# Sorting for top-k on one core: GpSimd's share of the second payloads goes to one half in the streams, and the products behind the softmax move to GpSimd and ScalarE

## The reference

```python
y = silu(x @ sg_w) * (x @ su_w) @ sd_w              # shared perceptron
for i in range(16):
    gate_feature = x * pe[i] @ gate_w + gate_b       # 625 x 768
    gate_weight, gate_idx = top_k(gate_feature, 384)
    gate_weight = softmax(gate_weight)
    gathered = take_along_axis(x, gate_idx)
    u = gathered * gate_weight
    y = y + silu(u @ eg_w[i]) * (u @ eu_w[i]) @ ed_w[i]
```

## Time and profile before

| | |
|---|---|
| median of 3 runs | 7316.7 us (7311.38 to 7317.13) |
| profiled execution | 7314.8 us |
| its span, first to last instruction | 7313.0 us |
| granted TensorE clock, mean | 0.938 |
| busy: PE, DVE, ACT, POOL | 6048.6, 5625.4, 2711.6, 3137.3 us |

### The profile page before, as it was taken

One profiled execution on the slowest core, in us unless ns is written; L12 is line 12 of the kernel. 1 busy time (PEld: TensorE's weight loads), 2 busy tenths in 40 slices (PEclk: granted clock), 3 DMA queues, 4 the chain that ended last, 5 costly groups with the idle time before them and its releaser, 6 DMA issues. The chain is left out here.

```text
span 7313.0 us, 76698 instructions
## 1 busy us (share of the span) xinstructions
PE 6048.6 (83%) x16985; PEld 3132.3 (43%) x16985; DVE 5625.4 (77%) x6713; ACT 2711.6 (37%) x4185; POOL 3137.3 (43%) x3512
## 2 busy tenths in 40 slices
PE   7989988888787878787878787878787878788888
PEld 5545544444343434343434343434343434344454
DVE  3011012999899989898999898999999999998860
ACT  0000000444444444444444444444444444444341
POOL 2233033545454545354545454545454545454440
PEclk9989999999999989899999899999999999999999
DMA  3355364000000000000000000000000000000101
GB/s 87 115 150 147 116 141 135 20 14 14 14 14 14 14 14 14 14 14 14 14 14 14 14 14 14 14 14 14 14 14 14 14 14 14 14 14 14 59 20 47
DMA packets 118210, 262.95 MB, mean 36 GB/s; under 512 B 39164, under 2 KB 49922, under 8 KB 117682
## 3 DMA queue, kind: packets, MB, share of 16 engines
q1 hardware_dynamic: 70322, 180.18, 6.9%
q0 software_dynamic: 47360, 77.17, 4.7%
HBM read 222.43 MB, written 34.58 MB: 35 GB/s over the span
## 5 line engine op out<-in xcount | busy, mean ns | idle before, releaser
L1107 PE MATMUL mask_ps<-key,neg_ident 125*125 125x480 f32 (+7 forms) x4128 | 1929.0, 588 | 717.8 <-DVE key L1383 711.5
L1309 ACT COPY mask_ps<-key 125x960 f32<-125x960 f32 (+7 forms) x1136 | 952.5, 838 | 1762.8 <-DVE pay L1425 1383.8
L1205 POOL TENSOR_TENSOR pay<-pay_rest,pay 125x360 int32<-125x360 int32 (+11 forms) x1104 | 882.0, 799 | 1472.8 <-DVE pay L1408 1471.0
L1107 PEld LDWEIGHTS mask_ps<-key,neg_ident 125*125 125x125 f32 x4128 | 745.0, 196 | 1680.7 <-DVE key L1383 1203.4
L1408 DVE COPY_PREDICATED pay<-mask_ps,pay 125x480 f32<-125x480 int32 (+5 forms) x1104 | 1229.8, 1114 | 116.8 <-PE mask_ps L1107 80.1
L1198 POOL TENSOR_TENSOR pay_rest<-pay 125x360 int32<-125x360 int32 (+11 forms) x1104 | 878.1, 795 | 812.4 <-DVE pay L1425 512.2
L1374 DVE TENSOR_TENSOR key<-mask_ps,key 125x480 f32<-125x480 f32 (+5 forms) x1104 | 1084.4, 982 | 40.4 <-PE mask_ps L1107 35.0
L1383 DVE TENSOR_TENSOR key<-mask_ps,key 125x480 f32<-125x480 f32 (+5 forms) x1104 | 1087.7, 985 | 8.3
L1107 PE MATMUL mask_ps<-key_top,neg_ident 125*125 125x480 f32 (+3 forms) x1472 | 613.7, 543 | 317.9 <-DVE key_top L1383 303.8
L1425 DVE COPY_PREDICATED pay<-mask_ps,pay_rest 125x600 f32<-125x600 int32 (+9 forms) x1104 | 832.2, 754 | 39.7
L1323 ACT COPY pay_rest<-pay 125x600 f32<-125x600 f32 (+9 forms) x1104 | 678.6, 615 | 425.3 <-DVE pay L1425 232.6
(11 more groups left out here) (178 smaller groups left out, 5855.2 us busy)
## 6 DMA issues: line engine op xcount, KB each, us to landing
w_rel<-L_gnn_W SPq DMA_DIRECT2D x16, 2304.0 KB, 23.4
w_exp<-L_ffn_ed_w SPq DMA_DIRECT2D x16, 2304.0 KB, 8.4
messages_dram<-y_out SPq DMA_DIRECT2D x16, 1875.0 KB
w_exp<-L_ffn_eg_w SPq DMA_DIRECT2D x16, 1152.0 KB, 5.3
w_exp<-L_ffn_eu_w SPq DMA_DIRECT2D x16, 1152.0 KB, 7.8
root_w<-L_gnn_root SPq DMA_DIRECT2D x2, 2304.0 KB
w_exp<-L_ffn_sg_w SPq DMA_DIRECT2D x4, 1152.0 KB, 5.8
w_exp<-L_ffn_su_w SPq DMA_DIRECT2D x4, 1152.0 KB, 8.5
```

The lines of the kernel that those rows point to most:

```text
L1107: last = pe.matmul(mask, neg_ident[0:TP, 0:TP], operand, start=False, stop=True, skip_group_check=True)
L1205: pool.tensor_tensor(second, shares(pay_was(u))[1].bitcast(I32), first, ALU.subtract).then_inc(pays_taken, 1)
L1309: act.copy(seed_of(u), compared(u)[0]).then_inc(seeded, 1)
```

## The change

Three edits. First, `shares` learns the unit and gives GpSimd 4/8 instead of 3/8 below `APART`; above it stays 3/8. Second, the five multiplications at the turn's end leave VectorE: GpSimd multiplies exponential by payload (`weigh`) at the beginning of the next turn, ScalarE multiplies by the inverted sum (`scale`) behind the seed of unit 4, and VectorE keeps only the reciprocal (`invert`), which goes ahead of unit 2 of the next turn. Third, the work beside the units starts at unit 4 instead of unit 1 (`WEIGH` is 3), since its inputs are ready only then.

```diff
-def shares(view):
+def shares(view, u):
     dim = next(d for d in range(1, len(view.shape)) if view.shape[d] > 1)
-    cut = view.shape[dim] - max(1, view.shape[dim] * 3 // 8)
+    eighths = 4 if UNITS[u][0] < APART else 3
+    cut = view.shape[dim] - max(1, view.shape[dim] * eighths // 8)
...
+        WEIGH = 3
...
-            for u in range(1, NU - 3):
+            for u in range(WEIGH + 1, NU - 3):
...
-                    spot = 1 + next(n for n, end in enumerate(ends) if end * whole >= made * passing)
+                    spot = WEIGH + 1 + next(n for n, end in enumerate(ends) if end * whole >= made * passing)
...
+            def weigh(e):
+                pool.wait_ge(pays_done, e * NU + NU)
+                pool.wait_ge(pays_taken, e * SUMS[NU] + SUMS[NU])
+                for t in range(NT):
+                    pool.wait_ge(exp_ready, e * NT + (t + 1))
+                    pool.tensor_tensor(mlp_in[:, t, :], mlp_in[:, t, :], last_pays[:, 0:KTOP, t],
+                                       ALU.mult).then_inc(weighted, 1)
...
+            def scale(e):
+                act.wait_ge(inv_ready, e + 1)
+                for t in range(NT):
+                    act.wait_ge(weighted, e * NT + (t + 1))
+                    act.activation(mlp_in[:, t, :], mlp_in[:, t, :], ACT.Copy,
+                                   scale=exp_sum[:, t:t + 1]).then_inc(u_ready, 1)
...
+            def invert(e):
+                dve.wait_ge(exp_ready, e * NT + NT)
+                dve.reciprocal(exp_sum[:, :], exp_sum[:, :]).then_inc(inv_ready, 1)
+
             def sort(i, last_one=False):
                 for u in range(1, FIRST[APART]):
+                    if u == WEIGH - 1 and not (isinstance(i, int) and i == 0):
+                        invert(i - 1)
                     larger_keys(i, u)
...
-                dve.wait_ge(exp_ready, i * NT + NT)
-                dve.reciprocal(exp_sum[:, :], exp_sum[:, :]).then_inc(inv_ready, 1)
-                dve.wait_ge(inv_ready, i + 1)
-                dve.wait_ge(pays_done, i * NU + NU)
-                dve.wait_ge(pays_taken, i * SUMS[NU] + SUMS[NU])
-                settle(dve, sort_waits)
-                for t in range(NT):
-                    dve.scalar_tensor_tensor(mlp_in[:, t, :], mlp_in[:, t, :], exp_sum[:, t:t + 1],
-                                             last_pays[:, 0:KTOP, t], ALU.mult, ALU.mult).then_inc(u_ready, 1)
```

More of the change, by code:

```diff
@@ L1196, in add_pays @@
                     pool.wait_ge(pays_taken, i * SUMS[NU] + SUMS[NEEDS[u]])
-                first, second = [shares(side)[1].bitcast(I32) for side in payloads(u)[0:2]]
-                pool.tensor_tensor(shares(pay_was(u))[1].bitcast(I32), first, second, ALU.add).then_inc(pays_added, 1)
+                first, second = [shares(side, u)[1].bitcast(I32) for side in payloads(u)[0:2]]
+                pool.tensor_tensor(shares(pay_was(u), u)[1].bitcast(I32), first, second, ALU.add).then_inc(pays_added, 1)
             def take_pays(i, u):
-                first, second = [shares(side)[1].bitcast(I32) for side in payloads(u)[0:2]]
+                first, second = [shares(side, u)[1].bitcast(I32) for side in payloads(u)[0:2]]
                 pool.wait_ge(moved, i * MOVES[NU] + (MOVES[u] + 1))
                 pool.wait_ge(pays_added, i * SUMS[NU] + (SUMS[u] + 1))
-                pool.tensor_tensor(second, shares(pay_was(u))[1].bitcast(I32), first, ALU.subtract).then_inc(pays_taken, 1)
+                pool.tensor_tensor(second, shares(pay_was(u), u)[1].bitcast(I32), first, ALU.subtract).then_inc(pays_taken, 1)
+            def weigh(e):
[5 more added lines that the diff above has]
+                                       ALU.mult).then_inc(weighted, 1)
             def sort(i, todo):
+                if not (isinstance(i, int) and i == 0):
+                    weigh(i - 1)
                 for u in range(NU):
@@ L1213, in sort @@
                         take_pays(i, ahead)
+                    if u == WEIGH and not (isinstance(i, int) and i == 0):
+                        pool.wait_ge(weighted, i * NT)
                     if SHARED[u]:
@@ L1322, in copy_pays @@
                 else:
-                    act.copy(shares(pay_was(u))[0], shares(first)[0]).then_inc(pay_copied, 1)
+                    act.copy(shares(pay_was(u), u)[0], shares(first, u)[0]).then_inc(pay_copied, 1)
+            def scale(e):
[4 more added lines that the diff above has]
+                                   scale=exp_sum[:, t:t + 1]).then_inc(u_ready, 1)
             def sort(i, todo, last_one=False):
@@ L1327, in sort @@
                     seed(i, u + 1)
+                    if u == WEIGH and not (isinstance(i, int) and i == 0):
+                        scale(i - 1)
                     copy_pays(i, u)
@@ L1421, in second_pays @@
                     elif SHARED[u]:
-                        smaller, mask, was = [shares(side)[0] for side in (smaller, mask, was)]
+                        smaller, mask, was = [shares(side, u)[0] for side in (smaller, mask, was)]
                     dve.wait_ge(moved, i * MOVES[NU] + (MOVES[u] + 1))
@@ L1450, in sort @@
                 second_pays(i, NU - 1)
[L1451 to L1459 removed]
             larger_keys(0, 0)
             smaller_keys(0, 0)
[L1463 removed]
+            sort(0)
+            with dve.Fori(1, NEXP - 1) as i:
                 sort(i)
             sort(NEXP - 1, last_one=True)
+            invert(NEXP - 1)
 def output(nc, ffn, tiles, chunks, ident, ones, x1_dram, y_tok, m1, m1_loaded, out):
```

6 lines of the change are left out of this document (4 added, 2 removed).

## The result

The changed kernel takes 7275.8 us (median of 4 runs, 7263.2 to 7280.8), the kernel before 7316.9 in the same comparison (7311.4 to 7322.9). The ratio is 0.9935, with a 95% interval of 0.9922 to 0.9948: faster by 0.65%. The forecast was 7220 us. The time lies inside the range of 7150 to 7285 and on the foretold side, but 56 us above the number.

What follows compares the result with a forecast made beforehand. VectorE was taken to bound 15 of 16 turns, TensorE mostly the last. Terms -3.3 - 5.2 + 0.5 + 0.7 + 0.8 = -6.5 us a turn, -97 over 15, +1 in the last: 7220 us, range 7150 to 7285.

Steps and rivals of the forecast that it cites:

- the share: Second payloads in the streams (units 0 to 55): GpSimd's larger part saves VectorE 5.8 us a turn, 5.2 counted.
- the products start later: Perceptron work from unit 4: +0.5 us denser products, +0.7 low clock at the start, +0.8 GpSimd late, each turn.
- the turn's end, with what moves: Between turns: 6.27 us falls to a 2.7 us seed wait; less the reciprocal, 3.3 us saved at 15 ends.
- Turn 0: First pass of the expert loop, counted among the 15 turns that were each to lose 6.5 us.
- The last turn: Sixteenth pass, mostly TensorE's: payloads' saving -3 us, products lost to its first steps +4, together +1.
- VectorE's work: Per turn: second payloads 5.8 us less, five multiplications (4.16 us) gone, reciprocal of 0.19 us kept.
- New operations on GpSimd and ScalarE: Turn's start: five GpSimd products at 1.0 us, five ScalarE scalings at 0.474, all hidden, GpSimd even at twice the price.
- The narrow place that I named: Unit 3's payload copy, queued behind ScalarE's five scalings: just hidden; at twice the price 2 us a turn.
- GpSimd late at unit 33: GpSimd's two `xs` tiles move from unit 30 to 32, making unit 33's first payload about 0.8 us late.
- The slower rival: Low clock reaches into the products, 3.5 us lost a unit; with five units more, 7480 us; chance 0.05.
- The rival with fewer low stretches: New order fills units without a product; a third of the 167.5 us of mask waits goes: 7164; chance 0.2.
- three signs of being wrong: VectorE waiting over 1 us for GpSimd in the streams, clock near 0.5 beyond unit 8, last turn over 408 us.

Runs made afterwards that it cites:

- e1: Kernel before with only the new share of one half for GpSimd in the streams; 7210.3 us, ratio 0.9835.
- e9: Kernel before with two extra unused matmuls in each unit where TensorE has no product; 7220.6 us, ratio 0.9866.
- e8: e1 with two extra unused matmuls in each unit where TensorE has no product; 7165.8 us, ratio 0.9784.
- e5: e1 with the perceptron's work started at unit 4 in all turns but the first, old turn's end kept; 7324.7 us, ratio 1.0002.
- e15: e5 with two extra unused matmuls in each unit where TensorE has no product; 7164.7 us, ratio 0.9788.
- e4: Changed kernel with turn 0 placing its perceptron work from unit 1 again; 7258.4 us, ratio 0.9904.
- e7: e4 with two extra unused matmuls in each unit where TensorE has no product; 7120.4 us, ratio 0.9722.
- e18: Changed kernel, turn 0 still late, with two extra unused matmuls in each unit where TensorE has no product; 7132.8 us, ratio 0.9732.
- e11: e7 with ScalarE making the next turn's unit 1 seed behind the first exponential instead of the fifth; 7121.1 us, ratio 0.9729.
- e13: e11 with two turns in VectorE's loop body, so half of the jumps are gone; 7102.7 us, ratio 0.9698.
- e6: e4 with the other turns' perceptron work started at unit 3 instead of unit 4; 7213.6 us, ratio 0.9851.
- e10: e4 with two extra unused matmuls in only six of the units without a product; 7201.1 us, ratio 0.9846.

## Why the prediction fell short

The runs give each term of the sum, in us of an ordinary turn (means of turns 1 to 14), once with the clock as the kernels leave it and once held (sums from the unrounded means):

| term | forecast | measured | at a held clock |
|---|---|---|---|
| the share | -5.2 | -6.8 (before to e1) | -3.5 (e9 to e8) |
| the products start later | +0.5 + 0.7 + 0.8 | +6.6 (e1 to e5) | 0.0 (e8 to e15) |
| the turn's end, with what moves | -3.3 | -3.6 (e5 to e4) | -3.6 (e15 to e7) |
| sum | -6.5 | -3.8 (before to e4) | -7.2 (e9 to e7) |

**The products start later: this step failed.** I charged 2.0 us for it: 0.5 for denser products, 0.7 for the low clock at the start and 0.8 for GpSimd. The mask waits further on I let stand as they were. Beside the share it costs 6.6 us: with the new order other units are empty, the clock is low at other products, and masks come late behind them. Proof is the pair e1 and e5 (+6.6 us a turn) beside e8 and e15 (none). The mask waits by themselves would mislead here. In an ordinary turn of the change they rose by 2.3 us (11.6 to 13.8), not far above the 1.8 that the forecast had allowed; the missing part is what the share alone gains by the clock (6.8 us, of which 3.5 remain at a held clock) and the late start takes away again.

**Turn 0: counted like the others.** Its products are others, and it grew by 12.4 us instead of falling by 6.5: 19 of the 58 us of the miss. Starting it early takes 21 us off it (e4); at a held clock the late start costs it 9.7 (e7 to e18).

**The last turn: a term too small.** It grew by 8.8 us instead of 1. The traces of the parts lay this to the late start: the turn takes 394.7 us before, 391.8 with the share alone, 403.4 with the late start alone and 403.5 with both (e5). I had given +4 for what a TensorE with little room loses. At a held clock e15 is still 8 us over e8, so this part is not the clock's.

**VectorE's work: right.** The second payloads and the multiplications were to take 5.8 us and 4.2, less 0.2 for the reciprocal, off a turn. VectorE's work fell from 336.5 to 326.95 us; by e1's 330.8 the share has 5.7 of it.

**The turn's end: right in size, half right in cause.** I forecast a wait of 2.7 us for the seed and read 2.68. e11 and e13 show that a second thing ends there too, the loop's branch. I had taken the multiplications for a cost only; they were also a cover.

**New operations on GpSimd and ScalarE: hidden, but dearer.** GpSimd's products took 1.19 us each, not 1.0; ScalarE's scalings 0.60, not 0.47. Both are far from twice the price.

```profile
L1217 POOL TENSOR_TENSOR mlp_in<-mlp_in,pay_rest x80: 1176/1193/1216, 1650.0 to 7059.2; 125x384 f32<-125x384 f32 x80
L1347 ACT ACTIVATE mlp_in<-mlp_in,exp_sum x80: 597/600/615, 1663.8 to 7060.4; 125x384 f32<-125x384 f32 x80
```

The narrow place that I named does show in the trace: at unit 3's payload VectorE waits 0.81 us, in ten of 14 turns for ScalarE's copy behind the scalings. But e5, which has no scalings, waits 1.14 us there, so they are not its price. By my reading of the earlier trace rows the wait at unit 3 should have moved to unit 6; it stayed, and 0.71 us stand at unit 6 besides.

**GpSimd late at unit 33: the wait is there,** 1.25 us; in all, the waits for GpSimd rose by 0.9 us a turn against 0.8. It does not carry over into the time: at a held clock e15 waits 1.5 us a turn more for GpSimd than e8, less for masks and ScalarE, and its turn is as long.

**The share's nine tenths: too much.** I counted 5.2 of 5.8 us. At a held clock the share brings 3.5; from e9 to e8 waits for masks grow by 1.2 us and those for ScalarE's payload copies by 0.8. The 6.8 of e1 are more than the 5.9 by which VectorE's mean work fell; about half of them came from where the low clock happened to fall.

**The slower rival** had this mechanism, the low clock reaching into the products, and I left it at 0.05 as if it came whole or not at all. I argued against it from a stretch of the kernel before with the clock at 1.00, but that shows where the old order keeps TensorE busy, not what the new order does. The rival with fewer low stretches took the same thing with the other sign; e1 shows it (584 us low instead of 621, and a time 27 us under the 7237 that its parts gave). Two of my three signs of being wrong came up: a wait for GpSimd over 1 us in the streams (unit 33), and a clock of 0.50 beyond unit 8 (unit 46). Most ordinary turns took 358.4 us, where I had expected 351 to 356.

**The sum at a held clock.** There the change is worth 7220.6 - 7120.4 = 100 us with turn 0 started early, and 7220.6 - 7132.8 = 88 as it stands; the forecast was 97. That nearness is partly luck: the share brings 1.7 us a turn less than I counted, the late start 2.0 us less of a loss. Of the 100 us 41 are given back without the filling: it saves e4 138 us, and before only 97.

Open: why the ordinary turn of the changed kernel has the two lengths 358.4 and 351.1. The long turns from the third on have their low stretches at the same units, and the two short ones lack those at units 46 to 48, 72 and 82. A turn seems to hand its pattern on to the next, but no run tested that.

## What to carry to other kernels

Where TensorE is not the bound but makes something short that the bound engine waits for, look for the steps in which it has little to do, and for the granted clock just behind them: a change of order moves these, and may cost or bring more than the edit itself. Before forecasting such a change, hold the clock up with idle matmuls in both versions, or at least count its waits as unknown and not as fixed. Forecast turns at the loop's ends by themselves: here they made up 27 of the 58 us of the miss. And ask of each removed instruction what ran under it: here five multiplications had covered a loop's branch.

## What the hardware showed that I had not expected

- Adding 108 matmuls a turn to a kernel whose TensorE was busy 82% of the turn made it 138 us faster (e4 to e7), and the kernel before 97.
- A loop's branch leaves VectorE without instructions for 2.8 to 3.1 us. Work that it already has in its queue runs on meanwhile.
- Turns of one loop with the same work take 351.1 or 358.4 us (the change), 347.9 or 355 to 359 (e6), 348.0 or 355.0 (e10). In the change and e10 the same length comes many times in a row.
- The Trainium skill (TensorE: Matmul & The Clock Gate, HAM oscillation) describes an engine that waits between its bursts and begins each at the low rate. Here the row at 3220.8 us agrees, with TensorE busy 5.47 of 7.80 us ahead of a stretch at 0.50; turn 8 does not, with the same pauses and a clock of 1.00. What this case adds is that the price is paid at the product behind the pause and by another engine.
